# The shared expert of the last sequence computed in the combining pass, with the end of the first pass reordered and the zero scatters issued at the begin

## The chip, the cores and the metric

The kernel runs on one core of a Trainium2 chip. The metric is the device time of one execution in microseconds. The core has TensorE (PE; the loading of its stationary operand is shown apart as PEld), VectorE (DVE), ScalarE (ACT), GpSimd (POOL) and SyncE (SP, which here only issues DMAs). Each engine takes its own instructions in order, and waits between engines are semaphores.

## The reference

The input is 16 sequences of 512 tokens with 256 channels, in float32. Two layers are applied one after the other:

```python
x = x + layernorm(attn(layernorm(x)))      # attn: sigmoid(r) * wkv_scan(decay, first, k, v), then Wo
x = x + layernorm(moe(layernorm(x)))

# moe, for each token
scores = softmax(xt @ gate_w.T + gate_b);  top 2 of 8 experts, weighed by their scores
expert(e) = (silu(xt @ w1[e].T + b1[e]) * (xt @ w3[e].T + b3[e])) @ w2[e].T + b2[e]
shared    = (silu(xt @ ws1.T + bs1) * (xt @ ws3.T + bs3)) @ ws2.T + bs2
moe = sum of the two weighed experts + shared
```

An expert has 256 inner channels, the shared expert has 512. All weights and activations are float32; the kernel splits each operand of a matmul into a high and a low part (of the type float32r) and adds three products (high by high, low by high, high by low).

## The kernel before

The program has three parts, one after the other; each is a block of its own on all engines.

`first_pass` goes over the 16 sequences. For each it does the layernorm, the matmuls for k, v and r (`kvr`), the scans on DVE (`scans`) with their sums on POOL (`running_sums`), the quotient (`denominator`, `invert`, `gate`), the split into `g_high` (ACT) and `g_low` (POOL), the output matmul (`project`), a layernorm and the residual (`add_x`, POOL), the second layernorm, its transposes (`turn_xf`), the routing (`route`, `rank_experts`, `count_tokens`, `place`), and the scatter of the token rows to their experts' regions of the DRAM tensor `slots_x` (`send`: eight indirect DMAs of POOL a sequence, L1543). The shared expert stands here too. With q from 0 to 3 for the four blocks of 128 inner channels:

- `inner(s, par, q)` on PE: 12 matmuls of 512 columns into two PSUM tiles h1 and h3 (L642)
- `silu` on ACT (L901), `product` on DVE (L1149), `h_high` on ACT (L909), `h_low` on POOL (L1535)
- `outer(s, half)` on PE: 24 matmuls of 256 columns for half a sequence (L663); the stationary operand is 128 neighbouring tokens of h
- `read_y` on ACT and `store_y` on SP (L437): the result goes to the DRAM tensor `sum_y`, to which the experts' results are added later

Sequences overlap: round i of the loop does the first half of sequence i, the second of i−1 and the experts of i−2 and i−3. In each engine's `body` the order is written out by hand. For the last three sequences (13, 14 and 15, called THIRD, SECOND and LAST) each engine has a function `finish` with an order of its own, in which the pieces are called `late_inner`, `late_outer`, `late_product`, `late_low_h` (here on DVE, L1372), `late_silu` (L956), `late_h_high` (L966), `late_read_y`, `late_turn_xf`, `late_route`, `late_count`. After the last `place` DVE computes the tables of the expert tiles (`expert_ends` L1264 to L1274, `tile_bounds` L1286 to L1294, `tile_tables` L1304 to L1317). Behind them SP loads the weights of the first two tiles (L103) and the token rows of the first four (L95). POOL's `finish` ends with `begin_scatters`: eight indirect DMAs that add rows of zeros to spare rows of `sum_y`. They give the semaphores `y_stored` the counts from which the scatters of the expert tiles go on:

```python
for j in range(PAIR):
    pool.indirect_dma_start(out=shared_y[:, :],
                            out_offset=bass.IndirectOffsetOnAxis(ap=spare_at[:, p % 2, j:j + 1], axis=0),
                            in_=nobody[:, 0, 0:C], in_offset=None, compute_op=ALU.add)\
```

`expert_tiles` goes over 71 tiles of 256 rows, each of one expert: load, transpose, matmuls (L1778, L1794), and an accumulating scatter into `sum_y` (L1944). Its block begins only when every engine has come to the end of the first pass's block.

`combine` goes over 16 blocks of 512 tokens, with four buffers for the loads. SP loads a block of `sum_y` (L2016) and of the residual x1 (L2018). On PE `turn` transposes the gates (L2031) and `bias` multiplies them with the output biases (L2040), into the PSUM tile b_ps; the stationary operand of `bias` is every fourth column of a tile, since a partition holds four neighbouring tokens here. ACT copies the transposed gates (L2055). DVE's `add` sums b_ps and the block (L2084) and takes the statistics (L2087, L2091, L2095, L2096). POOL computes the scales (L2112, L2115), ACT normalises (L2063), POOL adds x1 (L2124) and ACT stores (L2071). Before, no weight and no activation of the shared expert is needed in this part.

## Time and profile before

| | us |
|---|---|
| median of 3 runs | 1110.96 (1108.74 to 1112.02) |
| the profiled execution | 1108.02 |
| its span in the trace | 1106.2 |
| PE busy | 982.5 (89%) |
| DVE busy | 879.5 (80%) |
| POOL busy | 779.7 (70%) |
| ACT busy | 561.6 (51%) |
| the first pass, until the first expert matmul group | 668.3 |
| the combining pass, from 1031.7 | 74.5 |

Busy time is an average over parts with different limits. The time of the span is a sum over the parts, so the table is to be read with the windows of each part, in which the engine that is busy all the time, or the wait that ends last, tells what sets the pace there. Times in the rows count from the span's begin.

### The profile page before, as it was taken

The numbers are of one execution on the slowest core, as the hardware profiler recorded it, in microseconds if no ns is written. First come the engines' busy times: TensorE is split into PE (matmuls) and PEld (weight loads), VectorE is DVE, ScalarE is ACT, GpSimd is POOL, SyncE is SP. The second block draws the span as 40 slices with busy tenths as digits, with TensorE's granted clock in tenths as the row PEclk, the third lists the DMA queues.
The fourth block names the chain that finished last, engine by engine and source line by source line (L and its number), as shares of the span: only waits on it lengthen the run. The fifth ranks groups of instructions, "written<-read, shape, count | busy, mean of one in ns | idle before, by whom it ended". The sixth has DMA issues, their size and how long they took to land. (4 is left out here: it accounts for less than half of the span.)

```text
span 1106.2 us, 23285 instructions
## 1 busy us (share of the span) xinstructions
PE 982.5 (89%) x6344; PEld 876.6 (79%) x6344; DVE 879.5 (80%) x2225; ACT 561.6 (51%) x1020; POOL 779.7 (70%) x790
## 2 busy tenths in 40 slices
PE   3658999999999999999999958999999999998462
PEld 3547788888888888888888847999999999998341
DVE  6788999999999999999988735767776776776586
ACT  4355566556655665566555613344443444443365
POOL 2353987787779777877797661758766676767488
PEclk9679999999999999999999987999999999999555
DMA  6222443444344434443441493987778878886797
GB/s 197 67 79 93 139 144 97 143 148 135 105 140 148 138 101 142 148 132 105 144 129 58 156 290 75 212 228 124 114 132 192 214 115 218 199 203 111 235 399 296
DMA packets 108661, 172.72 MB, mean 156 GB/s; under 512 B 13869, under 2 KB 76744, under 8 KB 108360
## 3 DMA queue, kind: packets, MB, share of 16 engines
q1 hardware_dynamic: 76120, 119.68, 33.9%
q0 software_dynamic: 27744, 36.72, 19.0%
q10 hardware_dynamic: 4752, 15.80, 3.7%
q8 instruction: 19, 0.31, 0.1%
q14 instruction: 26, 0.21, 0.1%
HBM read 173.53 MB, written 76.86 MB: 226 GB/s over the span
## 5 line engine op out<-in xcount | busy, mean ns | idle before, releaser
L1944 POOL DMA_INDIRECT sum_y<-e_y,e_row_at x142 | 224.8, 1583 | 43.3 <-issue 39.7
L1778 PE MATMUL e_h_ps<-e_z_hi,w_room 128*128 128x256 f32 x1136 | 218.2, 284 | 9.2 <-DMA w_room<-w_split 7.5
L1778 PEld LDWEIGHTS e_h_ps<-e_z_hi,w_room 128*128 128x128 f32 x1136 | 182.1, 191 | 13.2 <-issue 10.6
L1822 ACT ACTIVATE e_act_h<-e_h_ps,w_room 128x256 f32<-128x256 f32 x142 | 67.4, 474 | 191.4 <-PE e_h_ps L1778 175.4
L1778 PE MATMUL e_h_ps<-e_z_lo,w_room 128*128 128x256 f32 x568 | 160.3, 282 | 0.0
L1543 POOL DMA_INDIRECT slots_x<-f_xf,f_at x120 | 136.6, 1139 | 31.9 <-issue 31.9
L1794 PE MATMUL e_y_ps<-w_room,e_h_hi 128*128 128x256 f32 x568 | 117.9, 291 | 1.3 <-DVE e_h_lo L1868 1.1
L1861 DVE SCALAR_TENSOR_TENSOR e_h<-e_h_ps,w_room,e_act_h 128x256 f32<-128x256 f32 x142 | 67.8, 482 | 63.9 <-ACT e_act_h L1822 61.8
L1116 DVE RECIPROCAL f_den<-f_den 128x256 f32<-128x256 f32 (+1 forms) x49 | 109.2, 2233 | 0.5
L1778 PEld LDWEIGHTS e_h_ps<-e_z_lo,w_room 128*128 128x128 f32 x568 | 108.5, 191 | 0.0
L642 PE MATMUL f_h_ps<-f_f_hi,f_w_hi 128*128 128x512 f32 x224 | 92.2, 412 | 5.5 <-DVE f_h_room L1149 3.1
L1794 PEld LDWEIGHTS e_y_ps<-w_room,e_h_hi 128*128 128x128 f32 x568 | 92.2, 189 | 1.7 <-DVE e_h_lo L1868 1.3
L642 PE MATMUL f_h_ps<-f_f_lo,f_w_hi 128*128 128x512 f32 x224 | 88.0, 393 | 0.0
L642 PE MATMUL f_h_ps<-f_f_hi,f_w_lo 128*128 128x512 f32 x224 | 87.7, 391 | 0.0
L1511 POOL TENSOR_TENSOR f_num<-f_num,f_a_sum 128x512 f32<-128x512 f32 x32 | 41.9, 1308 | 64.8 <-DVE f_a_sum L1099 64.8
L1794 PE MATMUL e_y_ps<-w_room,e_h_lo 128*128 128x256 f32 x284 | 79.8, 281 | 0.0
L34 POOL TENSOR_TENSOR e_scratch<-e_scratch 128x1 f32<-128x1 f32 x71 | 24.8, 349 | 76.5 <-DVE e_y L1878 36.4
L1535 POOL TENSOR_TENSOR f_h_lo<-f_h_room,f_h_hi 128x512 fp32r<-128x512 f32 x56 | 71.6, 1292 | 0.7
L569 PE MATMUL f_k_ps<-f_z_hi,w_room 128*128 128x512 f32 x128 | 56.9, 445 | 13.2 <-issue 10.5
L1096 DVE TENSOR_TENSOR_SCAN f_b_sum<-f_ew,rows_room 128x512 f32<-128x512 f32 x32 | 65.0, 2033 | 0.0
L1878 DVE TENSOR_SCALAR e_y<-e_y_ps,e_gate 128x256 f32<-128x256 f32 x142 | 61.8, 476 | 1.0 <-PE e_y_ps L1794 1.0
L901 ACT ACTIVATE f_h_room<-f_h_ps,f_bias 128x512 f32<-128x512 f32 x56 | 38.4, 685 | 45.8 <-PE f_h_ps L642 45.7
(296 smaller groups left out, 2971.2 us busy)
## 6 DMA issues: line engine op xcount, KB each, us to landing
w_room<-w_split SPq DMA_DIRECT2D x73, 512.0 KB
w_room<-w_split SPq DMA_DIRECT2D x71, 514.0 KB
w_room<-w_split ACTq DMA_DIRECT2D x69, 512.0 KB
rows_room<-slots_x SPq DMA_DIRECT2D x71, 260.0 KB, 2.9
f_x_in<-x SPq DMA_DIRECT2D x16, 512.0 KB, 5.2
f_x_res<-x SPq DMA_DIRECT2D x16, 512.0 KB, 4.6
x_dram<-f_x_room SPq DMA_DIRECT2D x16, 512.0 KB, 2.9
sum_y<-f_y SPq DMA_DIRECT2D x32, 256.0 KB, 2.2
```

The source lines that it names most:

```text
L569: last = pe.matmul(out[:, :], w[:, which, part, c * P:(c + 1) * P], z, start=(part == HERE and n == 0), stop=(part == SHIFT and n == 2))
L642: last = pe.matmul(out[:, :], a[:, which, c, q * P:(q + 1) * P], b[p][:, c, :], start=(n == 0), stop=(n == 5))
L1096: dve.tensor_tensor_scan(b_sum[c][:, 1:T + 1], ew[:, c:c + 1].to_broadcast([P, T]), ek[c][:, :], 0.0, ALU.mult, ALU.add)
L1116: dve.reciprocal(den[c][:, at], den[c][:, at]).then_inc(rec_ready, 1)
L1535: pool.tensor_tensor(h_lo[:, q, :], h[q][:, :], h_hi[:, q, :].bitcast(F32), ALU.subtract)\
L1543: pool.indirect_dma_start(out=slots_x[:, :], out_offset=bass.IndirectOffsetOnAxis(ap=at[p][:, j, k:k + 1], axis=0), in_=xf_of(s, p)[:, j, ...
L1778: last = pe.matmul(h_ps[q][:, which, :], w13(p, q, part)[:, which, c, :], z[p % 2][:, c, :], start=(n == 0), stop=(n == 5))
L1794: last = pe.matmul(y_ps[p % 2][:, j, :], a[p % 2][:, q, j * P:(j + 1) * P], w2(p, part)[:, q, :], start=(n == 0), stop=(n == 3 * parts - 1))
L1822: act.activation(act_h[q][:, :], h_ps[q][:, 0, :], ACT.Silu, bias=bias(p, 0, q)).then_inc(silu_ready, 1)
L1861: dve.scalar_tensor_tensor(out=h[p % 2][:, q, :], in0=h_ps[q][:, 1, :], scalar=bias(p, 1, q), in1=act_h[q][:, :], op0=ALU.add, op1=ALU.mul ...
L1878: last = dve.tensor_scalar(y[p][:, j, :], y_ps[p % 2][:, j, :], gate[p][:, j:j + 1], None, ALU.mult)
L1944: pool.indirect_dma_start(out=dst[:, :], out_offset=bass.IndirectOffsetOnAxis(ap=row_at[p][:, j:j + 1], axis=0), in_=y[p][:, j, :], in_off ...
```

## The change

Four things are changed.

1. The shared expert of the last sequence is taken out of the first pass: its `late_inner`, `late_silu`, `late_product`, `late_h_high`, `late_low_h`, `late_outer`, `late_read_y` and `store_y`. It is computed in `combine`: `inner`, silu, product, h_high and h_low stand ahead of everything else there, and `outer` adds its matmuls to b_ps in the last `bias`. The weights, the biases and the split activations of the last sequence get memory that lasts until then. The rows of `sum_y` that the last sequence's result had filled are set to zero by one DMA of SP.
2. The order in the `finish` functions of PE, ACT, DVE, POOL and SP is another one.
3. In the loop's body h_low of q = 0 and 1 goes from POOL to DVE (`first_h_low`).
4. The eight zero scatters go from the end of POOL's first pass to its round 0. They have 32 rows each instead of 128.

The combining pass:

```diff
@@ -2036,12 +2030,48 @@
                     return
                 pe.wait_ge(gt_ready, s + 1)
                 wait(pe, summed, s - 1)
+                if s == LAST:
+                    pe.wait_ge(hlo_ready, LATE_DONE + Q)
                 for j in range(SUBS):
-                    last = pe.matmul(b_ps[s % 2][:, j, :], gt[s % 2][:, :].rearrange("g (p j) -> g p j", j=SUBS)[:, :, j], b_out[:, :],
-                                     start=True, stop=True)
+                    last = pe.matmul(b_ps[s % 2][:, j, :], rows_of(gt[s % 2][:, :], j), b_out[:, :], start=True, stop=s != LAST)
+                    if s == LAST:
+                        last = outer(b_ps[s % 2][:, j, :], j)
                 last.then_inc(b_done, 1)
 
-            for i in range(-1, tiles):
+            def rows_of(cols, j):
+                return cols.rearrange("g (p j) -> g p j", j=SUBS)[:, :, j]
+
+            def inner(q):
+
+                for which, to, read in ((0, h1_ps, silu_ready), (1, h3_ps, h_ready)):
+                    pe.wait_ge(read, DONE + q)
+                    n = 0
+                    for c in range(CC):
+                        for a, b in ((w13["hi"], f_hi), (w13["hi"], f_lo), (w13["lo"], f_hi)):
+                            last = pe.matmul(to[:, :], a[:, which, c, q * P:(q + 1) * P], b[:, c, :],
+                                             start=(n == 0), stop=(n == 5))
+                            n += 1
+                last.then_inc(inner_done, 1)
+
+            def outer(to, j):
+
+                n = 0
+                for q in range(Q):
+                    for a, b in ((h_hi, w2["hi"]), (h_lo, w2["hi"]), (h_hi, w2["lo"])):
+                        n += 1
+                        last = pe.matmul(to, rows_of(a[:, q, :], j), b[:, q, :], start=False, stop=n == 3 * Q)
+                return last
+
+            turn(0)
+            inner(0)
+            turn(1)
+            inner(1)
+            bias(0)
+            inner(2)
+            turn(2)
+            bias(1)
+            inner(3)
+            for i in range(2, tiles):
                 turn(i + 1)
                 bias(i)
 
@@ -2070,7 +2100,27 @@
                 act.wait_ge(res_ready, s + 1)
                 act.dma_start(rows(out, s), res[s % DEPTH][:, :, :]).then_inc(stored[s % DEPTH], 16)
 
-            for i in range(-2, tiles + 2):
+            def silu(q):
+                act.wait_ge(inner_done, DONE + q + 1)
+                act.wait_ge(h_ready, DONE + q - 1)
...
+            def h_high(q):
+                act.wait_ge(h_ready, DONE + q + 1)
+                act.activation(h_hi[:, q, :], h[q][:, :], ACT.Copy).then_inc(hhi_ready, 1)
+
+            gates_turned(0)
+            silu(0)
+            gates_turned(1)
+            silu(1)
+            h_high(0)
+            silu(2)
+            h_high(1)
+            silu(3)
+            h_high(2)
+            h_high(3)
+            for i in range(0, tiles + 2):
                 gates_turned(i + 2)
                 normalise(i)
                 store(i - 1)
...
+            def product(q):
+                dve.wait_ge(silu_ready, DONE + q + 1)
+                dve.scalar_tensor_tensor(out=h[q][:, :], in0=h3_ps[:, :], scalar=shared_bias[:, 1, q:q + 1],
+                                         in1=act_h[q % 2][:, :], op0=ALU.add, op1=ALU.mult).then_inc(h_ready, 1)
+
+            def h_low(q):
+                dve.wait_ge(hhi_ready, DONE + q + 1)
+                dve.tensor_tensor(h_lo[:, q, :], h[q][:, :], h_hi[:, q, :].bitcast(F32), ALU.subtract).then_inc(hlo_ready, 1)
+
+            for q in range(Q):
+                product(q)
+                if q > 0:
+                    h_low(q - 1)
+            h_low(Q - 1)
             for i in range(tiles):
                 add(i)
```

PE's and DVE's order at the end of the first pass:

```diff
@@ -751,28 +744,22 @@
                 inner(THIRD, 1, 1)
                 outer(THIRD - 1, 1)
                 inner(THIRD, 1, 2)
+                project(LAST)
                 inner(THIRD, 1, 3)
                 late_turn_xf(SECOND)
-                project(LAST)
                 late_route(SECOND)
                 late_outer(THIRD, 0)
                 late_count(SECOND)
                 late_inner(SECOND, 0)
+                late_turn_xf(LAST)
                 late_outer(THIRD, 1)
+                late_route(LAST)
                 late_inner(SECOND, 1)
+                late_count(LAST)
                 late_inner(SECOND, 2)
-                late_turn_xf(LAST)
                 late_inner(SECOND, 3)
-                late_route(LAST)
-                late_inner(LAST, 0)
-                late_count(LAST)
                 late_outer(SECOND, 0)
-                late_inner(LAST, 1)
-                late_inner(LAST, 2)
-                late_inner(LAST, 3)
                 late_outer(SECOND, 1)
-                late_outer(LAST, 0)
-                late_outer(LAST, 1)
```

```diff
+                place(THIRD, 1)
                 product(THIRD, 0)
-                invert(LAST, 0, slice(0, T // 2))
-                invert(LAST, 0, slice(T // 2, T))
-                gate(LAST, 0, 2)
-                moments_x1(SECOND, 0)
-                product(THIRD, 1)
-                aggregate(LN_X1, SECOND, 0)
                 denominator(LAST, 1)
                 invert(LAST, 1, slice(0, T // 2))
-                product(THIRD, 2)
+                product(THIRD, 1)
                 invert(LAST, 1, slice(T // 2, T))
                 gate(LAST, 1, 4)
-                place(THIRD, 1)
-                late_f_low(SECOND)
-                product(THIRD, 3)
+                moments_x1(SECOND, 0)
+                product(THIRD, 2)
+                aggregate(LN_X1, SECOND, 0)
+                first_h_low(THIRD, 0)
+                first_h_low(THIRD, 1)
                 moments_o(LAST, 1)
                 aggregate(LN_O, LAST, 1)
+                product(THIRD, 3)
+                low_w(LAST)
+                late_f_low(SECOND)
                 add_gate_bias(SECOND, late_logits_ps)
+                moments_x1(LAST, 1)
                 add_low_logits(SECOND, late_logits_ps)
+                aggregate(LN_X1, LAST, 1)
                 rank_experts(SECOND)
                 read_counts(SECOND, late_before_ps)
                 place(SECOND, 0)
-                low_w(LAST)
-                moments_x1(LAST, 1)
                 late_product(SECOND, 0)
-                aggregate(LN_X1, LAST, 1)
-                spare_rows()
-                late_product(SECOND, 1)
                 late_f_low(LAST)
-                late_low_h(SECOND, 0)
-                late_product(SECOND, 2)
-                late_low_h(SECOND, 1)
-                late_product(SECOND, 3)
-                late_low_h(SECOND, 2)
                 add_gate_bias(LAST, late_logits_ps)
                 add_low_logits(LAST, late_logits_ps)
                 rank_experts(LAST)
-                late_low_h(SECOND, 3)
+                late_product(SECOND, 1)
                 read_counts(LAST, late_before_ps)
                 place(LAST, 1)
                 expert_ends()
-                late_product(LAST, 0)
-                late_low_h(LAST, 0)
+                late_low_h(SECOND, 0)
+                late_low_h(SECOND, 1)
+                late_product(SECOND, 2)
                 tile_bounds()
-                late_product(LAST, 1)
-                late_low_h(LAST, 1)
-                late_product(LAST, 2)
                 tile_tables()
-                late_product(LAST, 3)
-                late_low_h(LAST, 2)
-                late_low_h(LAST, 3)
+                late_low_h(SECOND, 2)
+                late_product(SECOND, 3)
+                late_low_h(SECOND, 3)
```

The loop's body on DVE, POOL's body and POOL's end, and SP's end:

```diff
@@ -1343,6 +1331,8 @@
                 product(i - 2, 1)
                 aggregate(LN_X1, i - 1, 1 - par)
                 low_w(i)
+                first_h_low(i - 2, 0)
+                first_h_low(i - 2, 1)
                 product(i - 2, 2)
                 denominator(i, 1)
...
@@ -1562,15 +1543,19 @@
                 send(i - 3, 1 - par, 1, (1, 2, 3))
                 inverse_std(LN_O, i - 1, 1 - par)
                 inverse_std(LN_X, i + 1, 1 - par)
+                if isinstance(i, int) and i == 0:
+                    begin_scatters(0)
+                    begin_scatters(1)
                 add_x(i - 1, 1 - par)
                 running_sums(i, 1)
                 inverse_std(LN_X1, i - 1, 1 - par)
                 if inside(i - 2, SEQS):
                     hold(pool, scratch, held, i - 2, (at_ready, i - 1))
                 send(i - 2, par, 0, (0, 1))
-                h_low(i - 2, 0)
-                h_low(i - 2, 1)
                 g_low(i, 0)
+                if isinstance(i, int) and i == 0:
+                    begin_scatters(2)
+                    begin_scatters(3)
...
@@ -1580,34 +1565,31 @@
                 h_low(THIRD - 1, 3)
                 send(THIRD - 1, 0, 1, (0,))
                 running_sums(LAST, 0)
-                send(THIRD - 1, 0, 1, (1, 2, 3))
+                send(THIRD - 1, 0, 1, (1,))
                 inverse_std(LN_O, SECOND, 0)
+                send(THIRD - 1, 0, 1, (2, 3))
+                make_nobody()
+                running_sums(LAST, 1)
                 add_x(SECOND, 0)
-                running_sums(LAST, 1)
                 g_low(LAST, 0)
-                inverse_std(LN_X1, SECOND, 0)
-                h_low(THIRD, 0)
-                h_low(THIRD, 1)
-                make_nobody()
-                h_low(THIRD, 2)
-                g_low(LAST, 1)
                 hold(pool, scratch, held, THIRD, (at_ready, THIRD + 1))
                 send(THIRD, 1, 0, (0, 1))
+                g_low(LAST, 1)
+                inverse_std(LN_X1, SECOND, 0)
+                send(THIRD, 1, 0, (2, 3))
+                h_low(THIRD, 2)
+                inverse_std(LN_O, LAST, 1)
+                send(THIRD, 1, 1, (0,))
+                add_x(LAST, 1)
                 h_low(THIRD, 3)
-                send(THIRD, 1, 0, (2, 3))
-                inverse_std(LN_O, LAST, 1)
-                send(THIRD, 1, 1, (0, 1))
-                add_x(LAST, 1)
-                send(THIRD, 1, 1, (2, 3))
                 inverse_std(LN_X1, LAST, 1)
+                send(THIRD, 1, 1, (1, 2, 3))
                 hold(pool, scratch, held, SECOND, (at_ready, SECOND + 1))
                 for k in range(2):
                     send(SECOND, 0, k, (0, 1, 2, 3))
                 hold(pool, scratch, held, LAST, (at_ready, LAST + 1))
                 for k in range(2):
                     send(LAST, 1, k, (0, 1, 2, 3))
-                for p in range(4):
-                    begin_scatters(p)
```

```diff
+            sp.dma_start(by_tiles(shared_y[LAST * T:SEQS * T, :]), nobody[:, :, 0:C].to_broadcast([P, SUBS, C]))\
+                .then_inc(late_zeros_stored, 16)
             store_y(THIRD, 0)
             store_x1(LAST, 1)
             store_y(THIRD, 1)
             clear_tails()
-            store_y(SECOND, 0)
 
             def first_rows(n):
                 load_rows(sp, tile_of, slots_x, n, early["rows"][n], early["rows_loaded"][n])
@@ -520,12 +511,12 @@
             sp.wait_ge(den_ready, 2 * SEQS)
             first_rows(0)
             first_rows(1)
-            store_y(SECOND, 1)
             first_weights(1)
             first_rows(2)
             first_rows(3)
-            store_y(LAST, 0)
-            store_y(LAST, 1)
+            store_y(SECOND, 0)
+            store_y(SECOND, 1)
+            sp.wait_ge(late_zeros_stored, 16)
             for p in range(2):
                 sp.wait_ge(x1_stored[p], 16 * (SEQS // 2))
```

## Rows read from the trace of the kernel before

**Rows 1.** The page's slices: PE's granted clock in tenths.
```profile
PEclk9679999999999999999999987999999999999555
```

**Rows 2.** Windows: width, busy of PE, PEld, DVE, ACT, POOL, clock, DMA, GB/s.
```profile
300.00:336.85 36.85, 36.85 (x212) 31.52 (x211) 33.96 (x80) 22.37 (x41) 29.83 (x33) 1.00 0.42 132
645.00:668.30 23.30, 6.39 (x52) 5.98 (x50) 2.93 (x10) 2.31 (x4) 11.70 (x9) 0.75 0.96 270
1031.70:1045.00 13.30, 10.39 (x39) 7.27 (x40) 9.03 (x29) 5.61 (x11) 3.89 (x6) 0.50 0.91 338
```

**Rows 3.** DVE in the loop: start, us, instruction, idle before, releaser.
```profile
335.71 0.75 DVE L1149 SCALAR_TENSOR_TENSOR f_h_room<-f_h_ps,f_bias,f_h_room 128x512 f32<-128x512 f32 x1 [1.40 <-ACT f_h_room L901]
```

**Rows 4.** POOL near the begin, in order of time.
```profile
41.21 1.90 POOL L1511 TENSOR_TENSOR f_num<-f_num,f_a_sum 128x512 f32<-128x512 f32 x1 [6.49 <-DVE f_a_sum L1099]
```

**Rows 5.** POOL at the first pass's end, in order of time.
```profile
642.45 0.96 POOL L1543 DMA_INDIRECT slots_x<-rows_room,f_at  x1 [0.30 <-issue]
...
658.47 1.55 POOL L1553 DMA_INDIRECT sum_y<-f_x_in,f_spare_at  x1 [3.12 <-DMA sum_y<-f_x_in,f_spare_at]
660.32 1.55 POOL L1553 DMA_INDIRECT sum_y<-f_x_in,f_spare_at  x1 [0.30 <-issue]
668.29 0.10 POOL L1949 MEMSET e_scratch<- 128x2 f32 x1 [6.42 <-POOLq L142]
```

**Rows 6.** DVE at the first pass's end, in order of time.
```profile
635.48 0.69 DVE L1372 TENSOR_TENSOR f_z_lo<-f_h_room,f_z_hi 128x512 fp32r<-128x512 f32 x1 [0.70 <-ACT f_z_hi L966]
...
645.72 0.22 DVE L1317 SCALAR_TENSOR_TENSOR tile_land<-f_num,f_land_base 1x70 int32<-1x70 f32 x1
```

**Rows 7.** SP's queue at the first pass's end, in order of time.
```profile
646.72 1.44 SPq L103 DMA_DIRECT2D w_room<-w_split  x3
```

**Rows 8.** DMA issues from 640 to 670: count, us to landing.
```profile
sum_y<-f_x_in,f_spare_at POOLq DMA_INDIRECT x8, 7.9
```

**Rows 9.** PE in its first dense stretch, in order of time.
```profile
16.72 0.63 PE L569 MATMUL f_k_ps<-f_z_lo,w_room 128*128 128x512 f32 x1
17.15 0.63 PE L569 MATMUL f_k_ps<-f_z_hi,w_room 128*128 128x512 f32 x1
...
22.02 0.39 PE L569 MATMUL f_v_ps<-f_z_hi,w_room 128*128 128x512 f32 x1
22.25 0.39 PE L569 MATMUL f_r_ps<-f_z_hi,w_room 128*128 128x512 f32 x1
```

**Rows 10.** PE in the combining pass, in order of time.
```profile
1031.79 1.88 PE L2031 MATMUL c_gt_ps<-eye,c_gates 128*27 128x128 f32 x8 [11.33 <-PEq L1635]
1033.59 1.31 PE L2040 MATMUL c_b_ps<-c_b_out,c_gt 27*128 27x256 f32 x4
1034.83 1.05 PE L2031 MATMUL c_gt_ps<-eye,c_gates 128*27 128x128 f32 x4
...
1090.44 1.30 PE L2040 MATMUL c_b_ps<-c_b_out,c_gt 27*128 27x256 f32 x4 [2.46 <-ACT c_gt L2055]
```

**Rows 11.** DVE in the combining pass, in order of time.
```profile
1035.69 1.23 DVE L2084 TENSOR_TENSOR c_acc<-c_b_ps,c_acc 128x1024 f32<-128x1024 f32 x1 [14.32 <-DMA c_acc<-sum_y]
...
1093.76 1.23 DVE L2084 TENSOR_TENSOR c_acc<-c_b_ps,c_acc 128x1024 f32<-128x1024 f32 x1 [0.58 <-DMA c_acc<-sum_y]
```

**Rows 12.** POOL's groups in the combining pass: busy us, mean ns | idle before.
```profile
L2124 POOL TENSOR_TENSOR c_res<-c_normal,c_x 128x1024 f32<-128x1024 f32 x16 | 37.6, 2350 | 0.0
L2112 POOL TENSOR_TENSOR c_rstd<-c_var,c_minus_half 128x4 f32<-128x4 f32 x16 | 16.3, 1018 | 13.7 <-DVE c_var L2096 13.7
```

**Rows 13.** ACT's groups at the first pass's end: busy us, mean ns.
```profile
L956 ACT ACTIVATE f_h_room<-f_turn_ps,f_bias 128x512 f32<-128x512 f32 x2 | 1.4, 690 | 0.9 <-PE f_turn_ps L713 0.9
L966 ACT ACTIVATE f_z_hi<-f_h_room 128x512 fp32r<-128x512 f32 x2 | 1.3, 631 | 7.9 <-DVE f_h_room L1366 7.9
```

**Rows 14.** PE at the first expert tile, in order of time.
```profile
671.49 0.63 PE L1778 MATMUL e_h_ps<-e_z_hi,w_room 128*128 128x256 f32 x2
671.92 0.41 PE L1778 MATMUL e_h_ps<-e_z_lo,w_room 128*128 128x256 f32 x1
```

167 lines of the change are left out of this document (91 added, 76 removed).

## The prediction

> **What bounds the kernel now.** I read the page's clock line first, then the table of windows, then the order of time engine by engine at the four places that the diff touches. The clock line shows full speed for nearly the whole span and half speed in its last three slices, which are the combining pass [rows 1]. The windows separate three regimes [rows 2]. In a period of the first pass's loop PE is busy 36.85 of 36.85 us, so the loop is PE's and the others matter only where they make PE wait. From 645.00 to 668.30 PE is busy 6.39 of 23.30 us, while the DMA engines are 0.96 busy: there the end of the first pass waits for tables and for transfers. From 1031.70 to 1045.00 the granted clock is 0.50 with PE busy 10.39 of 13.30 us. The expert tiles between are not touched by the diff; they move as a block.
>
> So the time changes at the program's begin, at the seam between first pass and expert tiles, at the first result of the combining pass and at its last. The four are in series: I price each and add.
>
> **The loop.** DVE takes over two h_low of a sequence. One costs 0.69 us on DVE [rows 6], so 1.38 us a period, and DVE stands idle 1.40 us exactly before the product that they are put ahead of [rows 3]. The cover is that wait for ACT's silu; POOL gets its time back and doesn't need it. I take 0. If the cover were gone, 14 periods by 1.38 us would be 19.3 us.
>
> **The begin.** The eight zero scatters go into POOL's first rounds. Two in a row start 660.32 − 658.47 = 1.85 us apart [rows 5], so the first four take 7.4 us. They stand ahead of the running sum for which POOL waits 6.49 us [rows 4]: 0.9 us sticks out, and the other four stand behind g_low, ahead of work that has slack of its own. Bounds 0 (the fill's first PE stage covers it) and 2; I take 0.5.
>
> **The end of the first pass.** Three things leave it. First, work: four products (0.75 each [rows 3]) and four h_low (0.69 each [rows 6]) of the last sequence leave DVE, of which two and two stood among the tables, and 96 matmuls leave PE, which waits there anyway. Second, order: on POOL the last running sum goes ahead of the residual's addition, on DVE the last reciprocals go ahead of two products. I carried this through, engine by engine, with the durations of before, once with every wait hidden and once with none: the last gate comes 4.3 to 2.7 us sooner, the last ranks 2.0 to 0 sooner, and the last table, now at 645.72 + 0.22 [rows 6], 4.8 to 2.8 sooner. Third, what stands behind the tables. POOL's last send ends at 643.41, and then the eight scatters run until 661.87, one with a wait of 3.12 us for an earlier one to land; the new block begins at 668.29, 6.42 us behind the last [rows 5]. With the scatters gone POOL is done at about 642.
>
> What is late next is the DMA work. The first weights are issued at 646.72 [rows 7], some 1 us behind the tables, and would now be at about 643. From there the first weights, rows and the last y come to about 3.1 + 1.0 + 0.5 = 4.6 MB (six weight pieces of 0.51 MB, four of rows, two of y); at the 270 GB/s of [rows 2] that is 17 us, so 660. The scatters took part in that rate, so without them 300 GB/s and 658 are possible. If the block's end waits for engines only, PE's last outer product and SP's last issue set it, at 651 to 653, with 2 us to the first matmul. So the new block begins at 653 (engines) or 657 to 661 (all transfers), against 668.3: a gain of 8 to 15. The 6.42 us between last scatter and new block are near the 7.9 us that a scatter takes to land [rows 8], which speaks for transfers being waited for, but for the scatters' own above all. I take 12, between the two.
>
> **The begin of the combining pass.** The first addition, at 1035.69 [rows 11], now stands behind the whole inner part of the shared expert. PE's order is turn(0), inner(0), turn(1), inner(1), bias(0), inner(2), turn(2), bias(1), inner(3). An inner part is 12 matmuls of 512 columns; at the low clock these start 17.15 − 16.72 = 0.43 us apart, at the high one 22.25 − 22.02 = 0.23, and in the kernel's first dense stretch the spacing changed from one to the other about 5.3 us in [rows 9]. So: inner(0) behind turn(0), a good microsecond into the stretch that begins at 1031.79 [rows 10], from 1032.9 (low) to 1038.0; turn(1) to 1039.0; inner(1) (high, 2.8) to 1041.9, bias(0) to 1043.1; inner(2) to 1045.9; turn(2) and bias(1) to 1048.1; inner(3) to 1050.9. Behind it silu 0.69 and h_high 0.63 on ACT [rows 13], product 0.75, h_low 0.69, 2.7 in all: the first addition at 1053.6, 18 us late. All at the high clock it would be 14 to 15, all at the low one 25.6 (three inner parts by 2.3 more, and the turns). I take 18, since 24 dense matmuls in a row are what raised the clock before. Nothing hides it: the first addition was held up by its own load until 1035.69 [rows 11], the loads lie ready long before 1053, and every later stage of the pass hangs on the additions in order.
>
> A part comes back. From first to last addition it takes 1093.76 − 1035.69 = 58.07 us [rows 11], 3.87 a block, where POOL's own work is 2.35 + 1.02 [rows 12] and a small one, 3.6 in all, and the waits are for loads, now four blocks further ahead. Bounds 0 and 2.5; I take 1.
>
> **The tail.** The last bias group starts at 1090.44 and its four matmuls take 1.24; the last addition starts only at 1093.76, 2.08 us behind them, since it waits for its load [rows 10, 11]. Now 48 matmuls of 256 columns stand in that group. With a contiguous stationary operand such matmuls start (671.92 − 671.49)/2 = 0.21 us apart at the low clock [rows 14]; the bias matmuls of this pass, whose stationary operand is read at every fourth column as the new ones' is, start (1034.83 − 1033.59)/4 = 0.31 apart [rows 10]. 48 × 0.21 = 10.2, 48 × 0.31 = 14.9; at the high clock throughout, half of the first, 5.1 to 5.8. Less the 2.08 the tail grows by 3.7, 8.1 or 12.8. The stride speaks for the long end, a rise of the clock on the way for the short one: I take 9.
>
> By the Trainium skill ("TensorE: Matmul & The Clock Gate", section "Step-by-step: what each phase is for") the time of a weight load goes by its number of columns alone; it names no price for a stride, so by it the tail would be 8.1, and the sum 1 us less. The pass's 0.31 us speaks against it.
>
> **The sum.** 0 + 0.5 − 12 + 18 − 1 + 9 = +14.5. The profiled execution took 1108.02 (span 1106.2), so the changed kernel's profile should show about 1122.5. The median of the runs before is 1110.96, 2.9 above the profiled one, which is taken as spread of runs; on the median's scale it is 1125. Differences under 0.3%, some 3.3 us, are about what a measurement here can't tell from none.
>
> **Rivals.**
> *H, the clock stays low* through the new work. For it: [rows 1] and [rows 2] show 0.50 for the whole pass with PE busy three quarters of its begin. Against it: the new stretch is much denser. Start 25.6, tail 12.8: 0.5 − 12 + 25.6 − 1 + 12.8 = +26, 1137. The Trainium skill ("TensorE: Matmul & The Clock Gate", section "HAM oscillation — how this bites in real kernels") says that groups of matmuls between waits are throttled again and again; by it the three inner parts, between which PE waits for silu and product, and the tail, would lean to this case. Chance 0.15.
>
> *F, faster.* The seam holds more than I give it: PE idles 17 of its 23 us. The mechanism is that the zero scatters' traffic, not the tables, delays weights and rows, and that the reordered end pulls the tables further than my hand count. It decides from the point at which the gain passes 26.5 + 3.3 = 30 us at my prices of the combining pass, or 22 at their low ends (14 + 5 − 1 + 3.3): the new block would have to begin at 646, 7 us ahead of the earliest begin by my count. With a gain of 24: 1111 − 24 + 0.5 + 14 + 4 − 1 = 1104.5. Chance 0.11, and 0.07 for a draw on the way there.
>
> *E, only engines are waited for*: gain 15, tail and start as taken: 1122. *N, all transfers are*: gain 8: 1129. Both lie in the main case, which has 0.62 together.
>
> *L, the loop stretches*, because the two h_low delay the product on which PE's buffers hang: up to +19, so 1144. Against it: the idle time is 0.02 us longer than what goes in. Chance 0.05.
>
> **How the numbers follow.** Main case 0.62, H 0.15, F 0.11, draw 0.07, L 0.05. Faster 0.11, same 0.07, slower 0.82. The main case's own range is 1116 (gain 15, start 14.5, tail 6) to 1133 (gain 8, start 18, tail 12.8). For 8 in 10 I take 1112 to 1137, which cuts off F and L and keeps H's point.
>
> **What the changed profile would show.** The first addition of the combining pass 17 to 19 us behind the first turn's 4, with matmul spacing 0.43 in inner(0) and 0.23 in inner(3); the group before the last addition 10 to 15 us long; no scatter between the last send and the new block, and the first expert matmul 8 to 15 us earlier; the loop's period 36.85 still. I would be wrong if the block began before 646, if the clock line showed half speed through the new stretches, if PE could take the inner parts while the pass's first loads still run, or if the period grew.

## The result

The changed kernel takes 1136.82 us (median of 4 runs, 1132.72 to 1140.44), the kernel before 1109.85 (4 runs, 1107.02 to 1112.02). The ratio is 1.0245, 95% interval 1.0216 to 1.0273: 27 us slower. The side was right, the size was not: I had forecast +14, and on the scale of the median from which the forecast was made the ratio gives 1138, just beyond the range of 1112 to 1137 (the measured median by itself lies at its very end). The profiled execution is the slowest of the four, 1140.44 with a span of 1138.7.

The span taken apart at five instructions of the two traces, beside the terms of the forecast:

| stretch | before | after | forecast | measured |
|---|---|---|---|---|
| to the first expert instruction of PE | 668.33 | 672.69 | −11.5 | +4.4 |
| from there to the first turn of the combining pass | 363.46 | 363.62 | 0 | +0.2 |
| to its first addition | 3.90 | 21.42 | +18 | +17.5 |
| to its last bias group | 54.75 | 53.71 | −1 | −1.0 |
| to its last addition | 3.32 | 14.77 | +9 | +11.5 |
| to the end | 12.44 | 12.49 | 0 | 0 |
| sum | 1106.2 | 1138.7 | +14.5 | +32.5 |

So one term failed by much, the end of the first pass (by 15.9 us), and the tail was 2.5 us short. The page's slice line and the windows of the loop, of the combining pass's begin and of its tail (columns as in [rows 1, 2]):

```profile
PEclk9779999999999999999988879999999999997655
```

```profile
300.00:336.85 36.85, 36.85 (x213) 31.61 (x211) 34.08 (x81) 22.34 (x41) 28.02 (x31) 1.00 0.42 132
1036.31:1057.73 21.42, 18.70 (x72) 14.19 (x72) 5.41 (x8) 6.47 (x11) 0.07 (x1) 0.86 0.50 196
1111.44:1126.21 14.77, 14.73 (x52) 12.87 (x52) 2.66 (x11) 4.16 (x8) 6.13 (x6) 0.50 0.47 184
```

The loop's period is 36.85 us with PE busy throughout, as in [rows 2]: two more h_low on DVE cost nothing there. DVE's busy time in the window rose by 0.12 us only, not by 1.38: one of the two gate multiplies (`gate`, f_g) of a period, which before ran beside POOL's h_low and g_low, took 2.01 us at 304.63 and takes 0.69 at 306.02 now. The new work at the combining pass's begin ran at a mean clock of 0.86, the tail at 0.50 although PE was busy 14.73 of 14.77 us.

**Where the two traces stand at 578 us.** The last matmuls of PE ahead of the first inner part of sequence 13, before and after:

```profile
577.88 0.63 PE L624 MATMUL f_shared_ps<-w_room 128*128 128x40 f32 x5
...
578.25 0.63 PE L615 MATMUL f_shared_ps<-w_room 128*128 128x40 f32 x5
```

**The end of the first pass.** PE after, in order of time, with every idle time of 1 us and more between 578 and the new block:

```profile
592.02 0.80 PE L633 MATMUL f_h_ps<-f_f_hi,f_w_hi 128*128 128x512 f32 x1 [5.97 <-DVE f_h_room L1128]
...
615.85 0.38 PE L681 MATMUL f_v_ps<-w_room,f_f_hi 128*128 128x16 f32 x1 [7.20 <-DVE f_f_lo L1346]
...
663.75 0.58 PE L729 MATMUL f_shared_ps<-f_w_hi,f_h_hi 128*128 128x256 f32 x1 [22.34 <-DVE f_h_lo L1359]
...
672.69 1.06 PE L1744 MATMUL e_turn_ps<-eye,rows_room 128*128 128x128 f32 x8 [1.64 <-PEq L142]
```

Before, PE's waits up to 632 were under 2 us each. Now it waits 5.97 us for the first product of sequence 13, 7.20 us for the low part of sequence 14 and 22.34 us for the last h_low. DVE, ACT and POOL say what stood ahead. First DVE ahead of the first product of 13 (L1128), before, after, and the same instruction of `place` in e7:

```profile
584.34 0.75 DVE L1149 SCALAR_TENSOR_TENSOR f_h_room<-f_h_ps,f_bias,f_h_room 128x512 f32<-128x512 f32 x1 [1.52 <-ACT f_h_room L901]
...
587.51 2.33 DVE L1211 TENSOR_TENSOR f_weighed<-f_chosen,f_gate_of 128x64 f32<-128x64 f32 x1
591.23 0.74 DVE L1128 SCALAR_TENSOR_TENSOR f_h_room<-f_h_ps,f_bias,f_h_room 128x512 f32<-128x512 f32 x1
...
590.19 0.23 DVE L1211 TENSOR_TENSOR f_weighed<-f_chosen,f_gate_of 128x64 f32<-128x64 f32 x1
```

The product comes 6.9 us later than before. Two reciprocals (577.36 to 580.72), a gate multiply and the `place` of sequence 13 stand ahead of it now, and `place` takes from 585.00 to 591.23, 6.2 us, where in e7 the same instructions take 2.4 (589.52 to 591.96). Some of them are slower in the one than in the other (2.33 against 0.23 us above), beside POOL's add_x, which runs from 587.42 to 589.75 after; that this is the reason isn't shown.

```profile
612.06 1.93 ACT L844 ACTIVATE f_on<-f_turn_ps,f_offset,f_rstd 128x256 f32<-128x256 f32 x4 [3.35 <-POOL f_offset L55]
613.87 0.61 ACT L941 ACTIVATE f_f_hi<-f_k_ps 128x512 fp32r<-128x512 f32 x1
...
652.47 0.69 ACT L946 ACTIVATE f_h_room<-f_h_ps,f_bias 128x512 f32<-128x512 f32 x1 [14.91 <-remote]
```

```profile
614.51 0.69 DVE L1346 TENSOR_TENSOR f_f_lo<-f_k_ps,f_f_hi 128x512 fp32r<-128x512 f32 x1 [4.16 <-ACT f_f_hi L941]
...
636.80 0.18 DVE L1190 TENSOR_TENSOR f_pos<-f_v_ps,count 128x32 f32<-128x32 f32 x1
...
660.69 0.22 DVE L1305 SCALAR_TENSOR_TENSOR tile_land<-f_num,f_land_base 1x70 int32<-1x70 f32 x1
```

```profile
627.70 0.99 POOL L1525 DMA_INDIRECT slots_x<-f_xf,f_at  x1 [0.16 <-issue]
...
649.60 0.96 POOL L1525 DMA_INDIRECT slots_x<-rows_room,f_at  x1 [0.30 <-issue]
672.65 0.10 POOL L1931 MEMSET e_scratch<- 128x2 f32 x1 [22.09 <-POOLq L142]
```

```profile
640.37 17.82 SPq L415 DMA_DIRECT2D slots_x<-f_x_in  x8
661.67 1.44 SPq L103 DMA_DIRECT2D w_room<-w_split  x3
```

ACT splits off the high part of sequence 14 only at 613.87, behind the normalising of the last sequence's output, for which it waited 3.35 us on POOL. The last gate multiply starts at 598.16 instead of 596.27, 1.9 us later where I had worked out 4.3 to 2.7 sooner. The last ranks are read at 636.80, not at 628.5 to 630.5 as I had worked out, and POOL's last send ends at 650.6, not at 642 (before: 643.4, [rows 5]). Then ACT waits 14.91 us ahead of the third silu of sequence 14 although its input lay ready (PE's inner parts of sequence 14 were done by 641.4); the trace calls the releaser "remote". The last table comes at 660.91, 15 us behind that of [rows 6], and the first weights are issued at 661.67 instead of 646.72 [rows 7]. The new block begins 22.09 us behind POOL's last send.

**The combining pass.** First matmuls of the first inner part, some of the second, and the first of the tail:

```profile
1036.31 1.03 PE L2025 MATMUL c_gt_ps<-eye,c_gates 128*27 128x128 f32 x4 [11.01 <-PEq L1617]
...
1037.56 0.63 PE L2051 MATMUL c_h_ps<-f_f_lo,f_w_hi 128*128 128x512 f32 x1
1037.99 0.63 PE L2051 MATMUL c_h_ps<-f_f_hi,f_w_lo 128*128 128x512 f32 x1
...
1043.73 0.40 PE L2051 MATMUL c_h_ps<-f_f_hi,f_w_lo 128*128 128x512 f32 x1
1043.96 0.40 PE L2051 MATMUL c_h_ps<-f_f_hi,f_w_hi 128*128 128x512 f32 x1
...
1111.44 0.60 PE L2036 MATMUL c_b_ps<-c_b_out,c_gt 27*128 27x256 f32 x1 [2.48 <-ACT c_gt L2085]
...
1112.36 0.44 PE L2062 MATMUL c_b_ps<-f_w_hi,c_h_lo 128*128 128x256 f32 x1
1112.60 0.44 PE L2062 MATMUL c_b_ps<-f_w_lo,c_h_hi 128*128 128x256 f32 x1
```

```profile
1057.73 1.22 DVE L2134 TENSOR_TENSOR c_acc<-c_b_ps,c_acc 128x1024 f32<-128x1024 f32 x1
...
1126.21 1.23 DVE L2134 TENSOR_TENSOR c_acc<-c_b_ps,c_acc 128x1024 f32<-128x1024 f32 x1 [12.01 <-PE c_b_ps L2062]
```

Inner part one runs at 0.43 us a matmul, the second at 0.23, as forecast; the first addition is 21.42 us behind the first turn instead of 3.90 [rows 10, 11]. The tail's matmuls start 1112.60 − 1112.36 = 0.24 us apart. A group of 12 with its bias matmul takes 3.67 us, which is 12 × 0.237 and 0.83 for the bias matmul between the others; as a group of four they stood 0.31 apart [rows 10]. The last addition waits for all four groups (14.77 us from the first group's start to it, 3.32 before).

### The profile page after: what moved, and what is told of

Its sections match the earlier page's. It is cut to its first block and busy times, and to the rows that moved or that the text cites. A ratio compares the mean times of both kernels' runs of the same rounds, so it can differ in the third digit from the quotient of the medians.

```text
span 1138.7 us, 23256 instructions
## 1 busy us (share of the span) xinstructions
PE 991.9 (87%) x6344; PEld 887.4 (78%) x6344; DVE 881.9 (77%) x2255; ACT 559.5 (49%) x1018; POOL 748.9 (66%) x763
## 5 line engine op out<-in xcount | busy, mean ns | idle before, releaser
L1760 PE MATMUL e_h_ps<-e_z_hi,w_room 128*128 128x256 f32 x1136 | 217.8, 282 | 11.6 <-DMA w_room<-w_split 9.8
L1525 POOL DMA_INDIRECT slots_x<-f_xf,f_at x120 | 127.3, 1061 | 29.3 <-issue 29.1
L633 PE MATMUL f_h_ps<-f_f_hi,f_w_lo 128*128 128x512 f32 x224 | 88.8, 397 | 0.0
L34 POOL TENSOR_TENSOR e_scratch<-e_scratch 128x1 f32<-128x1 f32 x71 | 21.4, 301 | 77.3 <-DVE e_y L1860 36.1
L799 ACT ACTIVATE rows_room<-f_k_ps 128x512 f32<-128x512 f32 x32 | 19.1, 598 | 91.2 <-PE f_r_ps L560 91.2
L888 ACT ACTIVATE f_h_room<-f_h_ps,f_bias 128x512 f32<-128x512 f32 x56 | 38.3, 684 | 52.0 <-PE f_h_ps L633 51.7
L1511 POOL TENSOR_TENSOR f_x_room<-f_on,f_x_res 128x1024 f32<-128x1024 f32 x16 | 38.5, 2404 | 38.6 <-ACT f_on L844 38.6
```

Of the source, the lines that this page charges most:

```text
L633: last = pe.matmul(out[:, :], a[:, which, c, q * P:(q + 1) * P], b[p][:, c, :], start=(n == 0), stop=(n == 5))
L1511: pool.tensor_tensor(x1[p][:, :, :], on[:, :, :], x_res[p][:, :, :], ALU.add).then_inc(x1_ready, 1)
L1525: pool.indirect_dma_start(out=slots_x[:, :], out_offset=bass.IndirectOffsetOnAxis(ap=at[p][:, j, k:k + 1], axis=0), in_=xf_of(s, p)[:, j, ...
L1760: last = pe.matmul(h_ps[q][:, which, :], w13(p, q, part)[:, which, c, :], z[p % 2][:, c, :], start=(n == 0), stop=(n == 5))
```

## The experiments

Each kernel was timed beside the kernel before, whose median moved between 1105 and 1110 us from one batch to the next; so ratios are compared, and traces by their own stretches. e1 to e4, e5 to e8 and e9 to e12 are three batches, each on a chip of its own. The changed kernel didn't move with the kernel before: its one run of e4 gives a ratio of 1.0250, that of e12 1.0285. So a difference of ratios across batches is not safe below some 0.4%, and kernels of one batch are compared first. "Block" is the first expert instruction of PE. The traces differ by up to 3 us already at the matmuls at 578 us, long before the seam, so the last column counts the block from there.

| | edit | median | ratio (95%) | last table | last send ends | block | block, from 578 |
|---|---|---|---|---|---|---|---|
| before | | 1109.85 | 1 | 645.9 | 643.4 | 668.3 | 90.4 |
| after | | 1136.82 | 1.0245 (1.0216 to 1.0273) | 660.9 | 650.6 | 672.7 | 94.4 |
| e1 | scatters only | 1098.94 | 0.9915 (0.989 to 0.994) | 648.9 | 646.4 | 660.0 | 80.7 |
| e2 | old orders | 1125.20 | 1.0174 (1.0128 to 1.022) | 640.3 | 643.1 | 655.5 | 78.5 |
| e3 | no late shared expert | 1107.93 | 0.9994 (0.9974 to 1.0013) | 650.5 | 654.1 | 666.4 | 89.0 |
| e4 | after, second run | 1135.80 | one run | 651.7 | 651.9 | 668.0 | 90.1 |
| e5 | break between sends | 1139.70 | 1.0328 (1.0297 to 1.0359) | 653.8 | 655.4 | 667.8 | 89.4 |
| e6 | e2 without a break | 1125.61 | 1.0192 (1.0165 to 1.0219) | 642.8 | 645.6 | 657.8 | 79.2 |
| e7 | product first | 1133.48 | 1.0271 (1.0233 to 1.0309) | 647.5 | 652.4 | 665.2 | 86.1 |
| e8 | contiguous h | 1132.64 | 1.0254 (1.0226 to 1.0281) | 651.7 | 655.8 | 668.8 | 88.8 |
| e9 | high part first | 1130.70 | 1.0235 (1.0189 to 1.0282) | 649.0 | 649.6 | 661.7 | 83.1 |
| e10 | both first | 1125.18 | 1.0188 (1.0149 to 1.0227) | 645.4 | 646.0 | 658.0 | 79.4 |
| e11 | spread | 1116.17 | 1.009 (1.0059 to 1.0121) | 641.8 | 644.6 | 656.8 | 79.0 |
| e12 | after, third run | 1137.47 | one run | 651.7 | 655.8 | 669.8 | 90.2 |

### The zero scatters alone

```diff
                 inverse_std(LN_X, i + 1, 1 - par)
+                if isinstance(i, int) and i == 0:
+                    begin_scatters(0)
+                    begin_scatters(1)
...
-                for p in range(4):
-                    begin_scatters(p)
```

> The kernel before with one part of the change: the eight zero scatters at the begin, with 32 rows. Theory S (the scatters cost what I gave them): the begin +0.5, and the new block of the expert tiles begins when the transfers have landed, about 660 to 664 instead of 668.3, since PE's last outer product still ends at 654 and the first weights are still issued at 646 to 647; total -4 to -8 us. Rival: the scatters filled time in which weights and rows had to arrive anyway, total -1 to +1.

```profile
660.00 1.06 PE L1771 MATMUL e_turn_ps<-eye,rows_room 128*128 128x128 f32 x8 [1.62 <-PEq L142]
```

The block begins at 660.0, 1.6 us behind PE's last outer product, although the tables came 3 us later than in the trace before. The kernel is 0.85% faster than before, some 9 us, a little beyond the upper end of what I expected. Its profiled execution is the slowest of its seven (1106.07), with 367.1 us in the experts, so the trace shows the gain of the seam (9.7 us, counted from 578) and the median that of the kernel. This is the fastest of all the kernels here, and it beats both.

### The old orders

```diff
 # finish() of PE, ACT, DVE and POOL
-<orders of the changed kernel>
+<orders of the kernel before, without inner, silu, product, h_high, h_low, outer, read_y of LAST>
```

> The changed kernel with the four old orders at the first pass's end, less the last sequence's shared expert (it stays in the combining pass); scatters at the begin and h_low in the loop as changed. Theory O (the new order makes PE wait 6 us for the product of sequence 13 and 7 us for the low part of 14, and so makes the tables late): last table at 642 to 645, new block at 657 to 661, total about 1111 + 29 - 9 = 1131 or, against the changed kernel, -5 to -14. Rival A (ACT's one wait of 14.9 us for nothing that the trace shows comes whatever the order): the wait is seen here too, new block at 668 or later, total as the changed kernel, +-3.

```profile
640.09 0.22 DVE L1305 SCALAR_TENSOR_TENSOR tile_land<-f_num,f_land_base 1x70 int32<-1x70 f32 x1
```

```profile
655.49 1.94 PE L1748 MATMUL e_turn_ps<-eye,rows_room 128*128 128x128 f32 x8 [18.38 <-PEq L142]
```

Theory O held, the table and the block both some 2 us sooner than it said, and rival A fell: ACT shows no wait for "remote" here and the total is 11.6 us below the changed kernel's. The last table comes 5.6 us sooner than before and the block at 655.5, 12.8 us sooner (12.0 counted from 578): that is the −12 of my sum. So the price that I gave the seam is that of a kernel with the old order; the new order by itself gives back 12 to 16 us (block at 90.1, 90.2 and 94.4 from 578 in the three runs of it, 78.5 here).

### The last sequence's shared expert left out

```diff
-            inner(0)
...
-                    if s == LAST:
-                        last = outer(b_ps[s % 2][:, j, :], j)
```

> The changed kernel with the last sequence's shared expert left out of the combining pass altogether, so that it is computed nowhere (the output lacks it for 512 tokens). If the trace's sum holds, the combining pass is as before: -17.5 at its begin, -11.5 at its end, +1 for waits, so -28 us against the changed kernel, 1108 to 1110; what is left against before is the seam, which then is 0 to +4. Rival: the pass is paced by its transfers, and the shared expert is partly hidden: -15 or less.

The kernel takes the time of before, 0.9994 (0.9974 to 1.0013), though it computes less, and the combining pass has the lengths of before: 3.63, 54.01 and 3.27 us where the table above has 3.90, 54.75 and 3.32. The late shared expert costs its full 28 us there (e4, the changed kernel's one run in this batch, is 27.9 us slower); nothing hides it. The seam came out a little better than the 0 to +4 that I expected (block at 666.4, 668.3 before).

### A second and a third run of the changed kernel

> The changed kernel unchanged, for a second look. If ACT's wait of 14.9 us ahead of the third silu of sequence 14 belongs to the program, it stands there again, within a us or two; if it is chance (its runs were 1132.7 to 1140.4), it is shorter or gone and the span is 1131 to 1135.

> A third look at the changed kernel, beside e8 and e5, whose first pass is the same or nearly so and showed no 'remote' wait on ACT. If that wait belongs to the program as it lies in memory, it stands here as in the two looks before (8 to 15 us in all); if it is chance, it can be missing.

```profile
643.20 0.69 ACT L946 ACTIVATE f_h_room<-f_h_ps,f_bias 128x512 f32<-128x512 f32 x1 [5.89 <-remote]
...
653.23 0.69 ACT L946 ACTIVATE f_h_room<-f_turn_ps,f_bias 128x512 f32<-128x512 f32 x1 [7.90 <-remote]
```

The rows are the second run's. There ACT waits twice for "remote", 13.8 us in all, before two silus of sequence 14, in e3 8.2 us, and 2.4 us in e1, which has the old order; in the third run and in e5 to e11 there is no such wait. The last table stood at 651.7 in both runs, 9 us sooner than in the first. So the program alone doesn't bring the wait about. All traces that show it are the first one and three of the four of the first batch, so whether it is chance or a matter of the chip isn't told. The block begins at 668.0 and 669.8 with it or without it: the first run's 14.9 us in one piece made it 3 to 5 us later, and it isn't what makes the kernel slower. What the wait is for stays open. One candidate is the loading of ACT's instructions; from 636 to 656 us the trace's instruction queue (q14) moves 2 pieces in the first run and 3 in the third, which tells nothing either way.

### POOL's chain of sends as its cause

```diff
+                for p in range(2):
+                    pool.memset(x_res[p][:, :, :], 0.0)
                 hold(pool, scratch, held, LAST, (at_ready, LAST + 1))
```

> The changed kernel with two memsets of 128x1024 on POOL (into buffers that are free) between the sends of sequence 14 and those of sequence 15; nothing waits for the memsets. Theory G (while POOL issues its scatters 0.30 us apart without a break, the other engines get their next instructions and SP's DMAs go out only now and then, and a break of 1 to 2 us lets them through): ACT's 'remote' waits before the silu of sequence 14 shrink from 8 to 15 us to under 4, SP's eight clears take about 10 us instead of 15 to 18, the last table comes 3 to 6 us sooner, total -2 to -6 us against the changed kernel. Rival (the wait belongs to the place in ACT's program, not to POOL): the waits stay, the sends end 2 us later, total 0 to +2.

> The kernel with the old orders (e2) with the same two memsets ahead of the sends of sequence 14, so that its 16 last sends stand without a break. Theory G: 'remote' or 'issue' waits of 4 us and more appear on ACT, SP's clears take 12 to 18 us, the last table comes 2 to 8 us later than 640.1, total +3 to +8 us against e2. Rival: the sends end 2 us later and nothing else happens, total 0 to +2.

e5's waits for "remote" are gone and SP's clears take 9.86 us, but the table came no sooner than in the third run, which has no such break either and no such wait. In e6 the same memsets stand ahead of the sends of sequence 14; it is as e2 with the block 2.3 us later, of which 1.7 stand there already at 578: no wait appears, the clears take 9.59 us. Theory G fell. By its ratio, 1.0328, e5 is even slower than the changed kernel. Of its batch, e8 is nearest; e5 is 7.1 us slower than e8, of which the tail is 5.0 (see below) and the two memsets take 1.86, so that what is left against 1.0245 belongs to the batch.

### Single steps of the new order undone

```diff
 # e7, DVE
                 denominator(LAST, 0)
-                invert(LAST, 0, slice(0, T // 2))
-                invert(LAST, 0, slice(T // 2, T))
                 read_counts(THIRD)
                 scans(LAST, 1)
+                product(THIRD, 0)
+                invert(LAST, 0, slice(0, T // 2))
+                invert(LAST, 0, slice(T // 2, T))
 # e9, ACT
+                late_f_high(SECOND)
                 normalise_o(LAST, 1)
-                late_f_high(SECOND)
```

> The changed kernel with one step of DVE's order undone: the first product of sequence 13 stands again ahead of the reciprocals of the last sequence. Theory O: PE's wait of 5.97 us at 592 shrinks to 1 to 2 us; the last gate comes 0.7 us later. If PE's lateness is what makes the ranks late, the last ranks come 2 to 4 us sooner and the total is -2 to -5 us. Rival: the chain through ACT's normalise and the low part of sequence 14 sets the ranks, so PE waits the more at 615: total -1 to +1.

> The changed kernel with one step of ACT's order undone: the high part of sequence 14 stands ahead of the normalising of the last sequence's output, for which ACT waited 3.35 us on POOL. Theory Q (the new order makes the ranks of sequence 14 late, by 13.5 us in the traces, and POOL's 16 last sends, 1.27 us each and in series, run on from there to 651 to 655, with the rows' loads behind them): PE's wait of 7.2 us ahead of the routing of 14 shrinks to 1 to 2 us, the sends of 14 start 5 to 6 us sooner and the last send ends at 645 to 649; total -3 to -6 us. Rival: the last sequence's ranks become late by as much, total -1 to +1.

> The changed kernel with the two steps undone together, DVE's (e7) and ACT's (e9). Theory Q: they act on the same chain one after the other, so their gains add: last send at 642 to 646, new block at 659 to 663, total -6 to -10 us against the changed kernel, some 5 us short of the kernel with all old orders (e2). Rival: the larger of the two alone.

PE ahead of the routing of sequence 14, in e7, e9 and e10:

```profile
613.36 0.38 PE L681 MATMUL f_v_ps<-w_room,f_f_hi 128*128 128x16 f32 x1 [7.18 <-DVE f_f_lo L1346]
```

```profile
592.36 0.79 PE L633 MATMUL f_h_ps<-f_f_hi,f_w_hi 128*128 128x512 f32 x1 [5.97 <-DVE f_h_room L1128]
...
611.92 0.28 PE L681 MATMUL f_v_ps<-w_room,f_f_hi 128*128 128x16 f32 x1 [2.94 <-DVE f_f_lo L1346]
```

```profile
608.72 0.30 PE L681 MATMUL f_v_ps<-w_room,f_f_hi 128*128 128x16 f32 x1 [2.94 <-DVE f_f_lo L1346]
...
658.04 1.07 PE L1744 MATMUL e_turn_ps<-eye,rows_room 128*128 128x128 f32 x8 [1.64 <-PEq L142]
```

Counted from 578, the routing of 14 starts at 37.6 to 38.3 us in the four traces with the new first pass (after, e4, e8, e12), and at 34.3, 33.3 and 30.1 in e7, e9 and e10. So the first step is worth some 3.6 us there, the second 4.6, both together 7.8. The last table follows: 651.7 in the undisturbed run, 647.5, 649.0, 645.4. The block follows as well: 86.1, 83.1 and 79.4 from 578 against 88.8 to 90.2. Against e12, the changed kernel's one run in their batch, e9 is 6.8 us faster and e10 12.3, a little more than expected; the ratios, 1.0235 and 1.0188 against 1.0245 from another batch, show 1 and 6 us. e7 has no run of the changed kernel beside it; it is 0.8 us slower than e8, whose tail is 5.0 us shorter, so an estimate from these is a gain of 4. e10 is 0.9 us short of e2, counted from 578, of the 11.7 between e12 and e2. Theory Q held, and the two steps make nearly all of the difference between the orders.

In e7, DVE's tables are ready at 647.5 and the weights are issued at once, but the rows wait for the last send:

```profile
648.24 1.44 SPq L103 DMA_DIRECT2D w_room<-w_split  x3
657.66 1.43 SPq L95 DMA_DIRECT2D rows_room<-slots_x  x2
```

The rows' loads stand at 657.66, 5.3 us behind the end of the last send (652.4), 9.4 us behind the weights. POOL's 16 last sends start 1.27 us apart at best, and from the first to the last it takes 21.9 us in the first run, 25.1 in the third and 26.2 in e7; the longest gap is the one behind the first send (4.0, 5.4 and 6.3 us, 3.2 before), and what fills it isn't told. They are the longer branch in the third run, in e7 and in e8. In e9 and e10 PE's last outer product ends 1.64 us ahead of the block and sets it.

### The stationary operand of the last matmuls

```diff
-                act.activation(h_hi[:, q, :], h[q][:, :], ACT.Copy)
+                act.activation(apart(h_hi[:, q, :]), together(h[q][:, :]), ACT.Copy)   # (j p) <- (p j)
...
-                        last = pe.matmul(to, rows_of(a[:, q, :], j), b[:, q, :], start=False, stop=n == 3 * Q)
+                        last = pe.matmul(to, a[:, q, j * P:(j + 1) * P], b[:, q, :], start=False, stop=n == 3 * Q)
```

> The changed kernel with the split h of the combining pass stored so that the four sets of tokens lie apart: ACT and DVE write at every 128th place, and the stationary operand of the 48 last matmuls is read contiguously. In the changed kernel these started 0.236 us apart, from first to last at the low clock. Theory R (the stride makes them slower, and the gaps that it leaves keep the clock from rising): spacing 0.213, and a rise to 0.118 within the stretch, so that the last addition comes 4 to 6 us sooner; total -4 to -6. Rival: the stride costs only the 0.02 us a matmul and the clock stays low: -1. Second rival: nothing, the spacing is set by something else.

```profile
1113.81 0.41 PE L2068 MATMUL c_b_ps<-f_w_hi,c_h_lo 128*128 128x256 f32 x1
1114.02 0.41 PE L2068 MATMUL c_b_ps<-f_w_lo,c_h_hi 128*128 128x256 f32 x1
...
1117.26 0.28 PE L2068 MATMUL c_b_ps<-f_w_hi,c_h_hi 128*128 128x256 f32 x1
1117.38 0.28 PE L2068 MATMUL c_b_ps<-f_w_hi,c_h_lo 128*128 128x256 f32 x1
```

Contiguous, the matmuls start 0.21 us apart, and from the second group on 0.12; from the tail's start (1112.89) to the last addition (1122.57) it takes 9.68 us instead of 14.77. In the ratio, 1.0254 against 1.0245 from another batch, those 5 us don't show; against e5 of its own batch it is 7.1 us faster. DVE's h_low, which now writes at a stride, takes 1.09 us instead of 0.68, which lengthens the pass's begin by some 0.5 us. Theory R has two halves, the stride and the clock, and one more trace parts them. In e6 (strided) the clock did rise within the tail, and it didn't help:

```profile
1105.00:1112.40 7.40, 7.34 (x28) 6.63 (x28) 0.02 (x1) 0.00 (x0) 0.00 (x0) 1.00 0.18 71
```

```profile
1107.35 0.40 PE L2068 MATMUL c_b_ps<-f_w_hi,c_h_hi 128*128 128x256 f32 x1
1107.58 0.40 PE L2068 MATMUL c_b_ps<-f_w_hi,c_h_lo 128*128 128x256 f32 x1
```

```profile
1107.44 0.33 PEld L2068 LDWEIGHTS c_b_ps<-f_w_hi,c_h_lo 128*128 128x128 f32 x1
...
1117.26 0.19 PEld L2068 LDWEIGHTS c_b_ps<-f_w_hi,c_h_lo 128*128 128x128 f32 x1
```

At a clock of 1.00 the strided ones start 1107.58 − 1107.35 = 0.23 us apart, as at the low clock before. The load of their stationary operand takes 0.33 us at that clock, the contiguous one in e8 0.19 (the last two rows). The strided load sets the pace, and the clock gives almost nothing back: e6's tail takes 14.15 us. At the low clock contiguous is 1.1 us better in 48 matmuls (0.213 against 0.237), so 4 of e8's 5.1 us need the high clock. Whether reading contiguously is what raised it isn't shown: of the nine strided tails one rose (e6) and eight stayed at 0.50, and of contiguous ones with this order there is one trace.

### The shared expert spread over the combining pass

```diff
             for i in range(-1, tiles):
                 turn(i + 1)
                 bias(i)
+                if i in (1, 3, 5, 7):
+                    inner((i - 1) // 2)
+                if 10 <= i < 14:
+                    pe.wait_ge(hlo_ready, LATE_DONE + Q)
+                    outer(late_b_ps[:, i - 10, :], i - 10)
```

> Old orders as in e2, the combining pass rearranged: additions begin at once; the four inner parts stand behind blocks 1, 3, 5 and 7, product and h_low an iteration or two behind, the four groups of 12 last matmuls behind blocks 10 to 13, contiguous as in e8, into PSUM of their own, which DVE adds to the last block in an addition of its own. PE has 3.77 - 2.36 = 1.4 us free a block at the low clock: the inner parts (5.1 each for two blocks) then cost 2.3 each, the outer ones 1.2 each, and the extra addition 1.2, some 15 in all; at the high clock next to nothing. So the pass costs +2 to +15 instead of +28, total 1125 - 26 to 1125 - 13, that is -9 to +4 us against before. Rival: DVE, with 3.3 us of work in 3.77, is pushed over by 1.4 us in eight blocks and sets the pace: +8 at least.

```profile
1029.10:1097.80 68.70, 51.98 (x201) 40.44 (x199) 57.83 (x163) 40.21 (x73) 45.51 (x39) 0.67 0.83 298
```

```profile
1044.79 1.05 DVE L2160 TENSOR_TENSOR c_h_lo<-c_h,c_h_hi 128x512 fp32r<-128x512 f32 x1 [0.19 <-ACT c_h_hi L2117]
...
1055.36 3.19 DVE L2160 TENSOR_TENSOR c_h_lo<-c_h,c_h_hi 128x512 fp32r<-128x512 f32 x1 [1.38 <-ACT c_h_hi L2117]
```

The first addition comes 5.92 us behind the first turn and the last 3.91 behind its bias group, but between them it takes 68.69 us instead of 54.75. That is +14 in the middle and 16.6 over the pass, a little beyond the 15 of the low clock; PE was busy 51.98 of 68.70 us at a mean clock of 0.67. DVE's h_low, which writes at a stride here, took 1.05, 3.19, 3.23 and 1.04 us instead of 0.68. Where it took 3.19, two additions stand 7.84 us apart (1050.63 and 1058.47) instead of 3.9, and h_low with its wait for ACT is 4.6 of it: DVE's own order held the additions up, as the rival said, and not PE's share alone. The kernel is 0.9% slower than before: the early block (656.8) is spent, and the total missed the range that I had given it.

## Why the prediction was off

**The loop, the begin**: right for the loop, with a help that I hadn't seen. The period is 36.85 us; the wait for ACT's silu took the two h_low in, and the shorter gate multiply gave back another 1.3 us a period. At 578 us PE is 0.4 us behind the trace before (forecast 0.5), but that is luck: the twelve other traces with the scatters at the begin stand between 0.9 us ahead of it and 2.2 behind.

**The begin of the combining pass**: right, 17.5 against 18, with the clock rising within the first inner part as worked out; e3, which leaves the late shared expert out, has both ends as before. Rival H, the low clock throughout, was wrong there. The waits gave back 1.0 us, as taken.

**The tail**: that it grows by its 48 matmuls was right, the size was short: 11.5 against 9. The 0.31 us of the bias matmuls did not carry over; with the spacing that was measured, 0.237, my formula gives 48 × 0.237 − 2.08 = 9.3. That this is near my 9 is luck, since I took 9 between a longer spacing and a clock that was to rise and shorten it, which with a strided operand it hardly does. The 2.1 us that are missing are the four bias matmuls: I counted them at 0.31 each, and between the others they take 0.83. By the rule of the Trainium skill ("TensorE: Matmul & The Clock Gate", section "Step-by-step: what each phase is for") the load of the stationary operand goes by its number of columns; here 128 columns take 0.33 us strided and 0.19 contiguous at the same clock, so the measurement decides against it where the columns are read at a stride.

**The end of the first pass**: this is the step that failed, in the sentence "I carried this through": "the last gate comes 4.3 to 2.7 us sooner, the last ranks 2.0 to 0 sooner, and the last table" ... "4.8 to 2.8 sooner". The gate came 1.9 us later, the ranks 6.3 later (636.80 against 630.52; 5.9 to 7.0 in the three runs, counted from 578) and the table, undisturbed, 5.7 later. From the ranks to the table it took 12.5 us in the third run instead of 15.4, 2.9 less, and that is the 2.8 that I had worked out; so the whole error lies ahead of the ranks. (I wrote that two products and two h_low stood among the tables; by the diff it was three products and two h_low, and an h_low pair and a product of sequence 14 stand there now.)

The gain of 12 for what is left out, for the scatters that went and for the seam behind it came with the old orders: the block begins 12.8 us sooner in e2, 12.0 counted from 578. That is in part luck, since the 12 had the reordered end's gain in it. e1 shows 9.7 of it for the scatters alone, counted from 578.

What I mis-read were two heads of queues. On DVE the reciprocals of the last sequence and the `place` of 13 now stand ahead of the first product of 13, which comes 6.9 us later and holds up PE's h3 tile for 5.97 us. On ACT the normalise of the last output ahead of the high part of 14 makes the routing of 14 wait for POOL's scales of 15. Undoing the one, the other and both brings the routing of 14 forward by 3.6, 4.6 and 7.8 us (e7, e9, e10). Sixteen sends of POOL at 1.27 us and more follow on the ranks of 14, a branch to which I gave no price because before it ended with the tables. I priced the new order for what it moves forward and not for what it puts behind.

Of the 32.5 us in the profiled execution, 3 to 5 are the long wait of ACT for "remote" (block at 672.7 against 668.0 and 669.8). How much of it is in the median isn't known: one of four executions was profiled, the slowest.
